# Moving five kinds of work between slots in a gated cross-attention kernel with a hand-written order

## What is computed

```python
x = x + tanh(g_xattn[0]) * attention(layernorm(x), ctx, Wq, bq, Wkv, bkv, Wo, bo)
x = x + tanh(g_ffn[0])   * mixture(layernorm(x), base_W, router_W, lora_A, lora_B)
```

## Time and profile before

| what | value |
|---|---|
| runs | 3, from 2304.1 to 2305.88 us, median 2305.09 us |
| the profiled execution | 2304.47 us |
| its span, from the first instruction to the last | 2302.4 us |
| PE busy | 2258.1 us, 98% of the span |
| DVE busy | 1814.8 us, 79% |
| ACT busy | 1667.8 us, 72% |
| POOL busy | 1630.0 us, 71% |

### The profile page before, as it was taken

One profiled execution on the slowest core, in us unless ns is written; L12 is line 12 of the kernel. 1 busy time (PEld: TensorE's weight loads), 2 busy tenths in 40 slices (PEclk: granted clock), 3 DMA queues, 4 the chain that ended last, 5 costly groups with the idle time before them and its releaser, 6 DMA issues.

```text
span 2302.4 us, 37405 instructions
## 1 busy us (share of the span) xinstructions
PE 2258.1 (98%) x12363; PEld 1938.1 (84%) x12363; DVE 1814.8 (79%) x3167; ACT 1667.8 (72%) x3152; POOL 1630.0 (71%) x1372
## 2 busy tenths in 40 slices
PE   7999999999999999999999999999999999999999
PEld 6888888887888888888888888888888888888875
DVE  5888888887887787787878787787787777787786
ACT  4777777776777777777777777777777777777773
POOL 5887886977668678757658678677757657667672
PEclk9999999999999999999999999999999999999999
DMA  7344353564233242425314333333423212222120
GB/s 261 128 158 138 115 165 108 173 199 155 88 112 111 95 160 95 133 79 206 97 42 138 115 131 110 109 134 121 156 79 105 92 60 99 77 88 90 55 109 37
DMA packets 137567, 271.85 MB, mean 118 GB/s; under 512 B 21664, under 2 KB 54944, under 8 KB 137120
## 3 DMA queue, kind: packets, MB, share of 16 engines
q1 hardware_dynamic: 122400, 255.71, 32.4%
q10 hardware_dynamic: 14976, 13.74, 2.7%
HBM read 202.44 MB, written 66.97 MB: 117 GB/s over the span
## 4 chain that ended last, share of the span: by engine, by line
PE 81%; DVE 8%; POOL 4%; issue 3%; ACT 3%; DMA 0%; ACTq 0%; SPq 0%; POOLq 0%; DVEq 0%
PE psW L438 12%; PE psW L440 12%; PE psW L439 12%; PE psS L438 7%; PE psS L440 7%; PE psS L439 7%; PE psW L664 7%; PE psW L665 7%; PE psW L666 7%; PE psW L494 3%; POOL xs L859 2%; DVE psum_ L1381 2%; DVE mrun L1348 2%; PE psW L502 1%; DVE pl L1118 1%
## 5 line engine op out<-in xcount | busy, mean ns | idle before, releaser
L859 POOL TENSOR_TENSOR xs<-xs,mb 128x512 f32<-128x512 f32 (+1 forms) x832 | 1066.3, 1309 | 474.2 <-ACT mb L930 474.2
L1348 DVE TENSOR_TENSOR mrun<-psS,mrun 128x512 f32<-128x512 f32 (+1 forms) x704 | 481.7, 684 | 340.5 <-ACT xs L930 338.8
L930 ACT ACTIVATE xs<-psS 128x512 f32<-128x512 f32 (+1 forms) x832 | 497.2, 598 | 244.1 <-PE psS L440 231.4
L1118 DVE TENSOR_TENSOR pl<-psP,ph 128x512 fp32r<-128x512 f32 (+1 forms) x672 | 458.4, 682 | 80.6 <-ACT ph L1060 75.6
L1060 ACT ACTIVATE ph<-xs 128x512 fp32r<-128x512 f32 (+1 forms) x832 | 518.8, 624 | 0.8 <-PE psW L666 0.8
L1381 DVE TENSOR_TENSOR psum_<-psP,psum_ 128x512 f32<-128x512 f32 (+1 forms) x672 | 455.9, 678 | 0.8 <-POOL pl L863 0.8
L1057 ACT ACTIVATE psP<-xs 128x512 f32<-128x512 f32 (+1 forms) x672 | 400.9, 597 | 29.3 <-DVE rinv L1281 12.7
L438 PE MATMUL psS<-ql,kh 128*128 128x512 f32 (+1 forms) x832 | 340.0, 409 | 6.3 <-DVE mrun L1348 5.2
L664 PE MATMUL psW<-ph,vh 128*128 128x512 f32 (+1 forms) x832 | 336.2, 404 | 3.3 <-POOL pl L863 3.1
L439 PE MATMUL psS<-qh,kh 128*128 128x512 f32 (+1 forms) x832 | 328.8, 395 | 0.0
L440 PE MATMUL psS<-qh,kl 128*128 128x512 f32 (+1 forms) x832 | 328.6, 395 | 0.0
(11 more groups left out here) (219 smaller groups left out, 4381.9 us busy)
## 6 DMA issues: line engine op xcount, KB each, us to landing
wqh<-scr_wq SPq DMA_DIRECT2D x96, 256.0 KB, 2.6
wql<-scr_wq SPq DMA_DIRECT2D x96, 256.0 KB, 3.0
woh<-scr_wo SPq DMA_DIRECT2D x47, 512.0 KB, 3.2
wol<-scr_wo SPq DMA_DIRECT2D x47, 512.0 KB, 4.3
rbc<-scr_r ACTq DMA_DIRECT2D x52, 256.0 KB, 3.3
scr_wq<-wqh SPq DMA_DIRECT2D x32, 256.0 KB, 2.0
scr_wq<-wql SPq DMA_DIRECT2D x32, 256.0 KB, 2.6
scr_wo<-woh SPq DMA_DIRECT2D x16, 512.0 KB, 2.6
```

What stands on the lines that cost most here:

```text
L859: eng.tensor_tensor(tile, tile, mb[0:rows_of(t), U % 2, :], ALU.subtract).then_inc(s_sub)
L930: return eng.activation(hi, src, ACT.Copy)
L1118: return eng.tensor_tensor(lo, src, f32(hi), ALU.subtract)
L1348: eng.tensor_tensor(run, psS[0:rows, s % 2, :], a, ALU.max).then_inc(s_m)
```

## The change

The division of the units V with V % 4 = 0 among those of `sum_by_mem` starts in slot 10 of unit V + 2, not 9. `sum_by_mem` leaves out V % 16 = 0 and 12, so these are eight units: 4, 8, 20, 24, 36, 40, 52 and 56. In units 14, 30, 46 and 62 (U % 16 = 14) the half p1 moves from slot 7 to slot 9. The second batch's `x` is turned in slots 1 and 2 of unit 15, not in slots 11 and 12 of unit 14, and the query half q0 of unit 15, which reads it, moves from slot 1 to 7; the third and fourth batch keep their places. The fourth cut of a context piece moves on POOL from slot 11 of unit 2 to the first slot of unit 2, and the fifth from slot 11 of unit 3 to slot 11 of unit 2, with their fetches on SP. The six instructions of the root move on DVE from slot 26 to slot 44, that is slot 5 of unit 3.

```diff
     def on_slot(V):
-        return 9 if sum_by_mem(V) else 8 if V < UN - 2 else 10 if V == UN - 2 else 6
+        return (9 if V % 4 else 10) if sum_by_mem(V) else 8 if V < UN - 2 else 10 if V == UN - 2 else 6
...
+    LAST_BUT_ONE = "m,v11 - b,v12 k2 p0 s k3 r q0 p1 q1 x0 o0,x1"
+    NEXT_X = "m x0 b,x1 k0 p1 s k1 q0 q1 k2 - o0 o1"
...
-                    UN - 1: "m - b - p1 s - r - - o0 - -"}.get(U, TURN if U > NU and U % NU == 2 else (AT_MEM if U >= MEM_LO + 2 else AT)[U % 4])
+                    NU - 1: NEXT_X, UN - 1: "m - b - p1 s - r - - o0 - -"}.get(U, TURN if U > NU and U % NU == 2 else LAST_BUT_ONE if U % NU == NU - 2 else (AT_MEM if U >= MEM_LO + 2 else AT)[U % 4])
...
-                if not 0 <= n < top or (kind == "x" and U % NU < 14):
+                if not 0 <= n < top or (kind == "x" and U not in (NU - 1, 2 * NU - 2, 3 * NU - 2)):
...
-        for t in (9, 11) if u == 1 else (11,) if u != 3 or U == 3 else ():
+        for t in (9, 11, 13) if U == 1 else (9, 11) if u == 1 else (11,) if u != 3 else ():
             if spare:
                 cuts[at + t].append(spare.pop(0))
...
-                if s == 26:
+                if s == 44:
                     inverse_dev(2, 2, NQ)
                     eng.tensor_scalar(rstds[:, 2:NQ], rstd[:, 2:NQ], SCALE, None, ALU.mult).then_inc(s_stat)
                     dve.wait_ge(s_stat, 1)
```

## The result

The changed kernel takes 2315.55 us, the median of five runs (2312.43 to 2317.52), where the kernel before takes 2305.09. The ratio is 1.0042, with a 95% interval of 1.0031 to 1.0054: slower by more than 0.2%, and 8.2 us over the forecast of 2307.3, outside the range given. The profiled execution took 2316.23 us with a span of 2314.2.

A forecast was written before the change was run, and what follows sets the result against it. It took PE, busy 98% of the span, to bound the kernel. Terms +3.8 + 1.4 - 0.4 - 2.6 = +2.2 gave 2306.7 us profiled, 2307.3 us as the runs' median, range 2299.0 to 2313.5.

The forecast's parts named there:

- The third units: Eight units with the division moved to slot 10: o0 in slot 12 0.47 us later each, +3.8 us in all.
- The wait of over a microsecond: In each unit with the division moved to slot 10, o0 in slot 12 waiting over a microsecond for `ol`.
- Units 2 to 4: Moved roots and context cuts: -2.1 in unit 2, +4.9 in unit 3, -1.4 in unit 4, together +1.4 us.
- five waits of 1.25: Unit 3: five of six root instructions each wait some 1.25 us for a POOL instruction; the maximum 4.2 us late.
- 0.7 lower: Unit 3: if only the three products among the root instructions surely wait for POOL, the sum is some 0.7 us lower.
- Units 14 and 15: Moved p1, `x` turns and q0: waits go, but POOL's later weight cut makes PE wait; together -0.4 us.
- the bound, +3: Units 14 and 15: upper bound of +3 us, with PE's half clock after both gaps.
- The 1.95: Unit 14: PE waits 1.95 us at slot 11's values, since POOL's late subtraction holds up ACT and `pl`.
- Units 30, 46 and 62: p1 moved to slot 9: bank wait goes, later output weight gives some back; -2.6 us, between -3.6 and -0.5.
- the rivals: Division units gain (0.14), POOL doesn't hold unit 14 (0.12), roots don't wait for POOL (0.14), roots become the cost (0.17).
- The upper end of the range: 2313.5 us: unit 3's roots wait two POOL instructions for each of five, the spread waits 9 us; chance 0.17.
- part 4: The forecast's term for units 30, 46 and 62, with p1 in slot 9: -2.6 us.

## Why the prediction was wrong

**The third units** went by the working. From unit 22's own start (786.09 instead of 784.38, 1.71 later), o0 starts at 818.58 where I had 818.49, and ACT's wait before `oh` is 1.48 for 1.4 forecast. The wait of over a microsecond that I had put before o0 is split: 0.55 before the values of slot 12 and 0.33 before o0. A unit costs 0.64 instead of 0.47, as the slot after it starts later too. I had left out that units 7 and 11 would lose over half of their own wait for POOL (0.71 and 0.92 before, 0.21 and 0.37 after).

```profile
816.48 0.69 ACT L1025 ACTIVATE oh<-psW,bkv_sb 128x512 fp32r<-128x512 f32 x1 [1.48 <-DVE psW L1325]
...
818.24 0.69 DVE L1122 TENSOR_TENSOR pl<-psP,ph 128x512 fp32r<-128x512 f32 x1 [1.20 <-ACT ph L1064]
...
820.29 0.47 PE L442 MATMUL psW<-wol,oh 128*128 128x512 f32 x1 [0.33 <-issue]
```

**Units 2 to 4** were right in each sign and each size within 0.7. PE's spread waited 2.47 for `rinv` (forecast 2.75) and the half clock came behind it, at 141.7. Walking along POOL's row gave nearly the right length, 4.04 us (134.83 to 138.87) where I had it 4.2 late. The count behind it was wrong: five waits of 1.25 would be 6.3. Four of the six waited. Two waited a whole POOL instruction (1.22, 1.23), two the rest of one (0.53, 0.54), and the reciprocal and the last (0.17) none; the last started while POOL was between two instructions.

The prediction used one rule of the Trainium skill, "SBUF — State Buffer", under "Who interferes with whom": that two SBUF inputs of VectorE and a reading GpSimd block each other. It left out that the same section also names `tensor_scalar`, in its two-port modes, among the instructions that can contend with GpSimd. The trace fits it, though no row tells the mode: L1180 is a `tensor_scalar`, with one SBUF input and two constants, and it took 1.23 us beside POOL and 0.17 beside an idle one. The prediction's "0.7 lower" doesn't follow either: by its own prices, two waits fewer would take off 2 x (1.25 - 0.17), some 2.2 us.

**Units 14 and 15**: POOL's row is as worked out. The cut starts at 530.35, which from the unit's start is 3.0 later than before, the last subtraction ahead of the exponential ends within 0.1 us of the forecast (42.26 after the unit's start for 42.30), and ACT, DVE and PE wait for it in turn:

```profile
539.28 2.08 POOL L917 TENSOR_SCALAR xraw<-xraw,mv,rstds 128x512 f32<-128x512 f32 x1
541.35 2.07 POOL L917 TENSOR_SCALAR cst<-cst,mv,rstds 128x512 f32<-128x512 f32 x1
...
544.71 0.60 ACT L1061 ACTIVATE psP<-xs 128x512 f32<-128x512 f32 x1 [2.56 <-POOL xs L863]
...
546.64 0.51 PE L668 MATMUL psW<-ph,vh 128*128 128x512 f32 x1 [1.45 <-DVE pl L1122]
```

What makes +1.9 of -0.4 is in the main the half clock in both units, which I had in the bound, +3, and not in the sum: PE is busy 1.5 and 1.6 us longer in them than with p1 in slot 7, where the clock is full. PE's waits in unit 15 come to 2.3 for 2.4 forecast. The 1.95 that I had put before slot 11's values of unit 14 did not come; in its place stand 1.81 before q1 in slot 10, which is the error of the next part.

**Units 30, 46 and 62 are the step that failed.** The prediction said: "The wait of 0.88 for the bank goes here too", and took -2.6 "between -3.6 and -0.5". The wait of 0.88 did go, in each of the three. What I did not ask is who waits for p1 to end. I asked it of POOL's cut in unit 14 and of SP's load of the output weight here, the two readers that the queues show; I did not ask it of ACT, whose `oh` overwrites what p1 reads. In the kernel before that wait is never seen, because p1 was always done in slot 7, so no row of the trace names it; it stood in the code, in the semaphore that `oh` waits for. PE waits 1.80 for it in unit 46, 1.81 in unit 30 and 2.72 in unit 62, where DVE's normalisation of 2.87 us comes in the way as well; units 30 and 62 have the half clock behind it. Against p1 in slot 8 that makes unit 46 2.0 and unit 30 3.5 us longer, and against the kernel before the three units are 5.9 longer, where -2.6 was forecast. The late output weight, the price that I did put in, was nothing: o0 does not wait for it, in slot 8 either. p1 in slot 7 takes the loss away in all three; in slot 8 units 30 and 46 are 1.1 under the kernel before, and unit 62 loses more, by another wait.

Of the rivals, none described this. The upper end of the range was made from the roots alone; a bound for part 4 above -0.5 would have needed a row for the wait that had none.

## What to carry to other kernels

When a reader of a buffer is moved later, look in the code, not in the trace, for who overwrites that buffer next: a wait that has always been met in time leaves no row. Price a moved job at each slot between its old place and the new one, since the gain of one step later can be whole while two steps turn it into a loss. And before a job is moved out of a stall's way, ask what other late engine it has been hiding.

## What was not expected of the hardware

The granted clock of PE doesn't follow from the idle before it alone. In unit 30 q1 waits 1.81 us in the changed kernel and 1.81 us in the kernel with the division in slot 9; in the first the 3.4 us from 0.3 us after that wait run at 0.50, the lower level of 1.2 GHz, and in the second at 1.00, the upper one. These two rows are the stretches behind the wait, the changed kernel's first:

```profile
1094.00:1097.40 3.40, 3.40 (x16) 3.11 (x15) 3.17 (x6) 0.79 (x2) 3.40 (x4) 0.50 0.61 227
```

```profile
1093.00:1096.40 3.40, 3.36 (x23) 3.08 (x24) 3.40 (x6) 2.11 (x5) 3.40 (x4) 1.00 0.57 206
```

PE starts 16 matmuls in the one and 23 in the other. In unit 46 of the changed kernel the same wait of 1.80 has no half clock after it. Unit 30 takes 39.11 us with the half clock and 37.59 without, so each is worth 1.5 us of scatter; these are single profiles, and they can't tell more. What decides it stays open.

The second is that beside an idle POOL a 6-column VectorE instruction takes 0.17 us, and beside a working one up to 1.23 here and 2.21 in the kernel before, while POOL's 512-column subtractions keep their 1.28 us: in these rows only VectorE pays.
